# Softmax sums of a 12-head attention: inverted as 12 turned columns a group instead of 324, with the step lists in a new order

## Chip, core and metric

One core of one Trainium2 chip runs the whole program. The metric is the device time of one execution in microseconds. The engines named below are TensorE (PE, with its weight loads PEld), VectorE (DVE), ScalarE (ACT), GpSimd (POOL) and SyncE (SP), which issues most of the DMAs. Each takes its instructions strictly in the order of its own queue.

## What is computed

A batch of 32 images with text goes through a patch embedding, a causal single-head attention with rotary positions, a 12-head attention and a mixture of eight experts of which each token takes two. There are T = 324 tokens of D = 192 features, in three tiles of 108, and heads of 16 features.

```python
h = _L0_tok_ref(x, L0_tok_W, L0_tok_b)                 # patches @ W.T + b
h = jnp.concatenate([h, txt], axis=1)
h = h + _L0_attn_ref(_layernorm(h, axis=-1), L0_attn_Wq, L0_attn_Wk, L0_attn_Wv)
h = h + _L0_ffn_ref(_layernorm(h, axis=-1), ...)
# in _L0_ffn_ref, the part that the change touches:
qkv = (xn @ qkv_w.T + qkv_b).reshape(Bx, Nx, 3, H, hd).transpose(2, 0, 3, 1, 4)
q, k, v = (qkv[0], qkv[1], qkv[2])
attn = jax.nn.softmax(jnp.einsum('bhqd,bhkd->bhqk', q, k) * scale, axis=-1)
o = jnp.einsum('bhqk,bhkd->bqhd', attn, v).reshape(Bx, Nx, C)
x = x + (o @ proj_w.T + proj_b)
```

## The kernel before

The program is a pipeline over the 32 images. A turn works on several of them at once: the front (embedding, first attention, the q, k, v of the second) on image b, the back (scores, softmax and values of the second attention) on b - 1, the close (projection, gate, positions, scatter to the experts) on b - 2, and from turn 19 on the experts on tiles of 256 gathered tokens, three a turn. Turns 0 and 1 fill the pipeline, turns 2 to 18 have no experts (list ATTEND_STEPS), turns 19 to 31 have them (list BOTH_STEPS), two more turns of that list drain the pipeline, and a tile stage (TILE_STEPS) does the experts that are left. Before turn 18 VectorE also makes the tables of tiles (`tables`).

The order in which steps are issued is written out by hand in these lists. Every engine walks the same list and issues those of its steps in that order; a step waits on semaphores for what it reads, and a TensorE step also until its PSUM banks (ATTEND_BANKS, BOTH_BANKS, eight banks) have been read by the step that FREED names. A step late on TensorE's queue therefore holds up all behind it.

For the second attention the 12 heads are three groups of four; in a group each head owns 32 partitions. `s` (18 steps of two heads and one tile of queries) computes scores so that `mx` on VectorE can take row maxima; `mt` transposes the maxima of a group (three transposes), `nm` on ScalarE scales them. `st` (18 steps) computes the transposed scores with the maxima subtracted; two neighbouring steps of `s` or `st` use the two halves of the array's rows and overlap. `ex` on ScalarE takes the exponential of each. `pv` (three steps, L1692) multiplies with the values: the result of a group is a bank of 128 x 324, in which the 32 partitions of a head hold 16 rows of output and then rows of softmax sums, since the padding of `Vp` is ones. `no` (L1239, VectorE) divides: a stream shuffle copies the rows of sums over the partitions of each head (L1246), a reciprocal inverts all 128 x 324 of them (L1248), and a multiply by the bank gives Os (L1251). The last `no` of an image is followed by its projection `pj` in the next turn (L1704), which adds three groups; `pj`'s bank is freed by `x1`.

Other steps named later: `tr1`, `tr2`, `tr3` (transposes of normalized rows), `he`, `n0`, `n1`, `xf` (VectorE), `qk2`, `v2` (TensorE, q and k and v of the second attention), `qkh` (ScalarE, two activations L921 and L922), `v2e` (ScalarE), `gate` (TensorE, products of eight columns), `gt1` (VectorE, 14 small operations of the gating), `pos`, `rs` (GpSimd, rotary sums), `X`, `W1`, `ge` (Gelu), `W2`, `yv` of the experts, `ld`, `ad`, `scat` (loads of tiles, adds and scatters by DMA).

Of the kernel before, what the change touches and what calls it, by code (L numbers as in the profile page):

```python
# [5 lines left out]
ALU = mybir.AluOpType  # L6
# [1890 lines left out]
```

## Time and profile before

| | us |
|---|---|
| median of 3 runs | 2734.13 |
| lowest to highest | 2730.55 to 2734.61 |
| profiled execution | 2737.74 |
| its span, first to last instruction | 2735.9 |

The profile is of one execution. Its page gives each engine's busy time and the chain of work that ended last; the trace behind it can be asked for a stretch. A row of waits says which engine stood still, for whose result, how long in total, how many times, and the longest. A wait put down to "issue" is one for nothing that the profile shows. Times in rows are microseconds from the start of the span, the mean of one instruction is in ns, and PEclk is the granted TensorE clock as a share of the full one.

### The profile page before, as it was taken

How to read it: one execution, taken by the hardware profiler on the slowest of the kernel's cores; microseconds unless marked ns; L12 is line 12 of the kernel's file. 1: busy time of each engine (PE TensorE's matmuls, PEld its weight loads, DVE VectorE, ACT ScalarE, POOL GpSimd, SP SyncE). 2: the span in 40 equal slices, each digit the busy share in tenths (PEclk: the TensorE clock that was granted, in tenths of full speed). 3: DMA queues.
4: the chain of work that ended last, by engine and by line, in shares of the span. 5: the costliest groups of instructions: out<-in, count | busy, mean ns of one | idle time of the engine just before them, and what ended most of it. 6: DMA issues, size and time to landing. Idle time of an engine off the chain costs nothing.

```text
span 2735.9 us, 62967 instructions
## 1 busy us (share of the span) xinstructions
PE 2434.0 (89%) x19692; PEld 1899.6 (69%) x19692; DVE 1616.2 (59%) x4054; ACT 1163.4 (43%) x2242; POOL 1043.0 (38%) x1196
## 2 busy tenths in 40 slices
PE   3979999999999998999999999999998778788876
PEld 2846666666666666677777777777776567677776
DVE  2347888888888888766666766666665211110110
ACT  1223344434434443455555555555555223323332
POOL 1112333333333333344444444444443344444444
PEclk9669999999999999999999999999999789989998
DMA  6511312231232224354444444454433356756673
GB/s 106 168 21 29 50 30 34 38 49 30 34 49 37 34 35 59 104 114 112 112 110 111 108 105 102 97 111 112 110 94 97 94 158 186 193 162 189 167 196 101
DMA packets 251812, 263.21 MB, mean 96 GB/s; under 512 B 36156, under 2 KB 231464, under 8 KB 251752
## 3 DMA queue, kind: packets, MB, share of 16 engines
q1 hardware_dynamic: 214888, 230.18, 35.2%
q0 software_dynamic: 36864, 32.27, 6.6%
q8 instruction: 34, 0.56, 0.1%
q14 instruction: 26, 0.21, 0.0%
HBM read 212.43 MB, written 52.83 MB: 97 GB/s over the span
## 4 chain that ended last, share of the span: by engine, by line
PE 67%; issue 10%; DVE 9%; DMA 5%; ACT 3%; POOL 3%; SPq 2%; DVEq 0%; ACTq 0%; POOLq 0%
PE PS L1545 43%; PE PS L1700 7%; PE PS L1689 5%; DMA B2t<-in_L_ffn_b 4%; PE PS L1616 3%; DVE rsi L1248 3%; PE PS L1666 3%; DVE MX L1236 2%; PE PS L1739 1%; PE PS L1675 1%; ACT XE L966 1%; POOL tmp L733 1%; POOL tmp L734 1%; PE PS L1577 1%; ACT pool L946 1%
## 5 line engine op out<-in xcount | busy, mean ns | idle before, releaser
L1236 DVE TENSOR_REDUCE MX<-PS 108x2 f32<-108x648 f32 x576 | 456.5, 823 | 66.4 <-PE PS L1666 61.8
L796 POOL DMA_INDIRECT out<-big,tokn x192 | 303.4, 1580 | 480.0 <-DVE big L1385 324.7
L946 ACT ACTIVATE pool<-PS 108x648 f32<-108x648 f32 x576 | 383.6, 713 | 192.8 <-PE PS L1689 167.0
L1545 PE MATMUL PS<-WB,big 128*128 128x192 f32 x2304 | 432.8, 345 | 2.8 <-ACT big L975 2.8
L1545 PE MATMUL PS<-XE,WF 128*128 128x256 f16 x2880 | 370.2, 283 | 58.8 <-ACT XE L966 46.5
L975 ACT ACTIVATE big<-PS,WF 128x256 f32<-128x256 f32 x576 | 241.3, 470 | 404.7 <-PE PS L1545 403.0
L1545 PEld LDWEIGHTS PS<-WB,big 128*128 128x128 f32 x2304 | 401.3, 203 | 15.6 <-issue 6.6
L1545 PEld LDWEIGHTS PS<-XE,WF 128*128 128x128 f16 x2880 | 278.8, 101 | 132.4 <-ACT big L975 42.2
L1385 DVE SCALAR_TENSOR_TENSOR big<-PS,grow,GB 128x192 f32<-128x192 f32 x192 | 71.1, 412 | 459.3 <-PE PS L1545 459.3
L774 POOL DMA_INDIRECT xbuf<-XR,DST x192 | 190.5, 992 | 255.8 <-issue 216.0
L1248 DVE RECIPROCAL rsi<-rsi 128x324 f32<-128x324 f32 x96 | 209.1, 2178 | 3.3
L1700 PE MATMUL PS<-pool,Vp 108*32 108x324 f32 x2304 | 201.6, 489 | 0.0
L1545 PE MATMUL PS<-tokW,ximg 96*88 96x192 f32 (+1 forms) x1024 | 193.7, 349 | 1.2 <-DVE b1s L1462 1.2
L784 POOL TENSOR_SCALAR GB<-B2t,grow 128x192 f32<-128x192 f32 x192 | 163.0, 1055 | 72.8 <-DVE grow L1396 71.4
L1545 PEld LDWEIGHTS PS<-tokW,ximg 96*88 96x88 f32 (+1 forms) x1024 | 185.3, 255 | 4.7 <-issue 1.4
L1666 PE MATMUL PS<-KH,QA 32*108 32x324 f16 x1152 | 155.4, 339 | 35.1 <-ACT Vp L931 10.0
L1689 PE MATMUL PS<-QA,KH 32*108 32x324 f16 x1152 | 157.8, 346 | 15.9 <-DVE MX L1236 13.5
L966 ACT ACTIVATE XE<-PS 128x768 f16<-128x768 f16 x96 | 77.8, 810 | 194.4 <-PE PS L1739 194.3
L937 ACT ACTIVATE NM<-PS 128x324 f16<-128x324 f32 x96 | 42.2, 440 | 254.5 <-PE PS L1675 254.4
L1666 PEld LDWEIGHTS PS<-KH,QA 32*108 32x108 f16 x1152 | 60.0, 121 | 125.4 <-DVE MX L1236 38.0
L1689 PE MATMUL PS<-QA,KL 32*108 32x324 f16 x1152 | 143.8, 310 | 0.0
L1689 PE MATMUL PS<-NM,big 32*108 32x324 f16 x1152 | 143.6, 309 | 0.0
(209 smaller groups left out, 4142.4 us busy)
## 6 DMA issues: line engine op xcount, KB each, us to landing
WF<-w1p SPq DMA_DIRECT2D x96, 771.5 KB
WB<-in_L_ffn_W SPq DMA_DIRECT2D x96, 576.0 KB
ximg<-in_x SPq DMA_DIRECT2D x96, 196.0 KB
XtR<-xbuf SPq DMA_DIRECT2D x96, 196.0 KB
ximg<-in_x SPq DMA_DIRECT2D x96, 195.1 KB
B2t<-in_L_ffn_b SPq DMA_DIRECT2D x96, 96.0 KB
out<-R SPq DMA_DIRECT2D x32, 243.0 KB
w1p<-WF SPq DMA_DIRECT2D x8, 768.0 KB, 6.3
```

The source lines that it names most:

```text
L774: nc.gpsimd.indirect_dma_start(xbuf[:, :], bass.IndirectOffsetOnAxis(ap=DST[:, NT * k + t:NT * k + t + 1], axis=0), XR[:, t, :], None).the ...
L784: last = nc.gpsimd.tensor_scalar(GB[:, i % 2, s_, :], B2t[:, i, :], grow[:, i, s_:s_ + 1], None, ALU.mult)
L796: nc.gpsimd.indirect_dma_start(rows_out, bass.IndirectOffsetOnAxis(ap=tokn[:, i, s_:s_ + 1], axis=0), Yt[:, i, s_, :], None, bounds_check= ...
L946: nc.scalar.activation(Pr[:, at:at + 2, :], pair(("st", p))[0:TP, :, 0:T], ACT.Exp, scale=SCALE2).then_inc(S["ex"], 1)
L966: nc.scalar.activation(XE[:, i, :, :].rearrange("p k t -> p (k t)"), bank(("X", i))[:, 0:384].bitcast(F16), ACT.Copy).then_inc(S["x_evac"], 1)
L975: last = nc.scalar.activation(hid[:, i, c, :], ps[:, TILE * (c % 2):TILE * (c % 2) + TILE], ACT.Gelu, bias=WF1[:, i, 2 * HID + c:2 * HID + ...
L1236: nc.vector.tensor_reduce(MX[:, qt, g, 64 * jj:64 * jj + 64:32], pair(("s", p))[0:TP, :, 0:T], AX.X, ALU.max).then_inc(S["mx"], 1)
L1248: nc.vector.reciprocal(at, at).then_inc(S["inv"], 1)
L1545: last = nc.tensor.matmul(out_ap, lhsT, rhs, start=(i == 0), stop=(i == len(products) - 1))
L1666: last = nc.tensor.matmul(ps[0:TP, i, 0:T], QA[r, g, TP * qt:TP * qt + TP], KH[r, g, :], start=True, stop=True)
L1689: last = nc.tensor.matmul(ps[0:TP, i, 0:T], left[r], right[r], start=n == 0, stop=n == 2)
L1700: last = nc.tensor.matmul(ps[32 * j:32 * j + 32, 0:T], Vp[:, kt, 4 * g + j, :], Pr[:, at, :], start=kt == 0, stop=kt == NT - 1)
```

## The change

`no` is split over four engines, once for each group. `oe` (ScalarE) copies the bank of `pv` to Os, which frees the bank. `sx` (TensorE) transposes the three tiles of 108 tokens of Os into a bank of its own, so that a sum stands once per token and head, in one column of each head. `ri` (VectorE) inverts those 3 x 4 columns on 108 partitions into RC. `rx` (ScalarE) writes each inverse 32 times side by side into RX (108 x 3 x 128). `bx` (TensorE) transposes RX back to 128 x 324 in a bank, and `no` (VectorE) multiplies it by Os. So a batch has 18 steps of these six kinds in place of three of `no`. The buffer `rsi` goes; the tile tables that borrowed it borrow Nrm instead, and `tables` waits for `tr2` of the turn before.

Both lists are in a new order, with new banks. Tile stage, loads, first attention, scores, exponentials and experts are computed as before. Cut to its core (the lists by the ends of both turns):

```diff
-    mx=18, sums=3, inv=3, no=3, x1=1, cx=1, ...
+    mx=18, oe=3, sx=3, ri=3, rx=3, bx=3, no=3, x1=1, cx=1, ...
 ATTEND_STEPS = [
...
+    ("n3",), ("tr3",), ("mt", 2), ("ex", 9), ("xh",), ("st", 10), ("xm",), ("rcp",), ("h1",), ("st", 11), ("gate",),
+    ("ex", 10), ("nm", 2), ("st1",), ("st", 12), ("st", 13), ("ex", 11), ("ex", 12), ("ex", 13), ("st", 14), ("is1",),
+    ("pv", 1), ("st", 15), ("gt1",), ("ex", 14), ("n1",), ("oe", 1), ("st", 16), ("st", 17), ("ex", 15), ("sx", 0),
+    ("ri", 0), ("pos",), ("tr2",), ("ex", 16), ("sx", 1), ("ex", 17), ("th",), ("tr2h",), ("xf",), ("ri", 1),
+    ("rx", 0), ("pv", 2), ("tr2l",), ("bx", 0), ("oe", 2), ("rx", 1), ("qk2", 0), ("xl",), ("no", 0), ("pos2",),
+    ("bx", 1), ("qk2", 1), ("qkh", 0), ("gt2",), ("scat",), ("hb",), ("qkh", 1), ("keep",), ("no", 1), ("sx", 2),
+    ("qkl", 0), ("ri", 2), ("rx", 2), ("qk2", 2), ("bx", 2), ("qkh", 2), ("qkl", 1), ("no", 2), ("v2",), ("v2e",),
+    ("qkl", 2),
 ]
...
+    ("gate",): (5,) ... ("sx", 0): (5,),
...
 BOTH_STEPS = [
...
+    ("qkh", 0), ("bx", 0), ("qk2", 1), ("no", 0), ("qkl", 0), ("ad", 2), ("qkh", 1), ("pv", 2), ("qk2", 2), ("rx", 1),
+    ("bx", 1), ("oe", 2), ("sx", 2), ("qkl", 1), ("ri", 2), ("qkh", 2), ("rx", 2), ("v2",), ("v2e",), ("qkl", 2),
+    ("bx", 2), ("no", 1), ("no", 2),
 ]
-         "qk2": "qkl", "v2": "v2e", "s": "mx", "mt": "nm", "st": "ex", "pv": "no", "pj": "x1", "tr3": "xm",
+         "qk2": "qkl", "v2": "v2e", "s": "mx", "mt": "nm", "st": "ex", "pv": "oe", "sx": "ri", "bx": "no", "pj": "x1", "tr3": "xm",
-        rsi = sb("rsi", [128, 2, T], F32)
+        RC = sb("RC", [TP, NT, HEADS], F32)
+        RX = sb("RX", [TP, NT, 128], F32)
+            def oe(b, g):
+                act.wait_ge(S["pv"], due("pv", b, g + 1))
+                act.wait_ge(S["pj"], due("pj", b - 1, 1))
+                nc.scalar.activation(Os[:, g, :], bank(("pv", g))[:, 0:T], ACT.Copy).then_inc(S["oe"], 1)
+            def rx(b, g):
+                act.wait_ge(S["ri"], due("ri", b, g + 1))
+                act.wait_ge(S["bx"], due("bx", b, g))
+                apart(act)
+                nc.scalar.activation(RX[:, :, :].rearrange("p t (j r) -> p t j r", j=4),
+                                     RC[:, :, 4 * g:4 * g + 4].rearrange("p t (j r) -> p t j r", r=1).to_broadcast(
+                                         [TP, NT, 4, 32]), ACT.Copy).then_inc(S["rx"], 1)
+            def ri(b, g):
+                dve.wait_ge(S["sx"], due("sx", b, g + 1))
+                dve.wait_ge(S["rx"], due("rx", b - 1, g + 1))
+                sums = bank(("sx", g))[0:TP, 0:384].rearrange("p (t j r) -> p t j r", t=NT, j=4)[:, :, :, HD]
+                nc.vector.reciprocal(RC[:, :, 4 * g:4 * g + 4], sums).then_inc(S["ri"], 1)
             def no(b, g):
-                nc.vector.stream_shuffle(at, ps, [16 + i % 16 for i in range(32)]).then_inc(S["sums"], 1)
-                nc.vector.reciprocal(at, at).then_inc(S["inv"], 1)
-                nc.vector.tensor_tensor(Os[:, g, :], ps, at, ALU.mult).then_inc(S["no"], 1)
+                dve.wait_ge(S["bx"], due("bx", b, g + 1))
+                nc.vector.tensor_tensor(Os[:, g, :], bank(("bx", g))[:, 0:T], Os[:, g, :], ALU.mult).then_inc(S["no"], 1)
-                dve.wait_ge(S["no"], due("no", attended, 3))
+                dve.wait_ge(S["tr2"], due("tr2", turned_, 1))
+            def sx(turn, b, g):
+                pe.wait_ge(S["oe"], due("oe", b, g + 1))
+                free(pe, turn, ("sx", g))
+                ps = bank(("sx", g))
+                for t in range(NT):
+                    last = nc.tensor.transpose(ps[0:TP, 128 * t:128 * t + 128], Os[:, g, TP * t:TP * t + TP], ident)
+                last.then_inc(S["sx"], 1)
+            def bx(turn, b, g):
+                pe.wait_ge(S["rx"], due("rx", b, g + 1))
+                free(pe, turn, ("bx", g))
+                ps = bank(("bx", g))
+                for t in range(NT):
+                    last = nc.tensor.transpose(ps[:, TP * t:TP * t + TP], RX[:, t, :], ident[0:TP, 0:TP])
+                last.then_inc(S["bx"], 1)
```

## Rows read from the trace of the kernel before

**Rows 1.** The page: busy time by engine, and the chain that ended last.

```profile
PE 2434.0 (89%) x19692; PEld 1899.6 (69%) x19692; DVE 1616.2 (59%) x4054; ACT 1163.4 (43%) x2242; POOL 1043.0 (38%) x1196
PE 67%; issue 10%; DVE 9%; DMA 5%; ACT 3%; POOL 3%; SPq 2%; DVEq 0%; ACTq 0%; POOLq 0%
```

**Rows 2.** Stretches by stage: us, busy by engine, clock, DMA share, GB/s.

```profile
213.10:1075.90 862.80, 807.33 (x6851) 569.78 (x6849) 734.23 (x1743) 355.34 (x720) 287.11 (x380) 0.95 0.25 38
1075.90:1139.70 63.80, 53.37 (x431) 38.33 (x429) 54.18 (x132) 22.21 (x45) 21.21 (x27) 0.87 0.60 143
1139.70:1999.40 859.70, 833.73 (x7298) 656.94 (x7297) 587.51 (x1482) 478.48 (x863) 381.39 (x429) 0.99 0.47 106
2136.00:2735.90 599.90, 472.20 (x3280) 427.12 (x3280) 75.23 (x324) 180.10 (x382) 267.27 (x233) 0.88 0.59 163
```

**Rows 3.** The same view of single turns: two of ATTEND, one of BOTH.

```profile
541.92:594.71 52.79, 49.39 (x431) 35.30 (x429) 46.05 (x110) 22.21 (x45) 18.19 (x24) 0.97 0.25 39
...
648.00:702.30 54.30, 50.99 (x431) 35.85 (x429) 45.94 (x109) 22.21 (x45) 18.19 (x24) 0.94 0.25 38
...
1283.62:1354.86 71.24, 69.10 (x611) 54.37 (x609) 49.22 (x125) 39.90 (x73) 32.11 (x37) 1.00 0.47 107
```

**Rows 4.** Waits of TensorE's weight loads, 213.1 to 1075.9 us (16 ATTEND turns).

```profile
PEld PS L1689 <- DVE MX L1236: 20.8, 48, 0.6
...
PEld PS L1545 <- DVE tmp L1196: 3.8, 16, 0.2
...
PEld PS L1689 <- ACT pool L946: 3.0, 16, 0.2
```

**Rows 5.** The same waits, 1139.7 to 1999.4 us (12 BOTH turns).

```profile
PEld PS L1577 <- ACT pool L946: 9.0, 12, 0.9
...
PEld PS L1675 <- DVE Os L1251: 7.8, 12, 0.7
...
PEld PS L1700 <- DVE MX L1236: 0.2, 1, 0.2
```

**Rows 6.** VectorE's groups by line: shapes, count, busy us, mean ns, idle before.

```profile
L1248 DVE RECIPROCAL rsi<-rsi 128x324 f32<-128x324 f32 x96 | 209.1, 2178 | 3.3
...
L1246 DVE STREAM_SHUFFLE rsi<-PS 128x324 f32<-128x324 f32 x96 | 50.1, 522 | 1.1 <-issue 0.4
...
L1251 DVE TENSOR_TENSOR Os<-PS,rsi 128x324 f32<-128x324 f32 x96 | 47.6, 496 | 3.3
...
L1212 DVE RECIPROCAL nm<-nm 108x3 f32<-108x3 f32 x32 | 5.4, 170 | 0.0
```

**Rows 7.** TensorE in order of time, BOTH: start, us, instruction.

```profile
1328.17 0.44 PE L1675 MATMUL PS<-cst,MX 108*128 108x108 f32 x3
1328.55 0.34 PE L1666 MATMUL PS<-KH,QA 32*108 32x324 f16 x2
...
1353.29 0.41 PE L1545 MATMUL PS<-qkvWa,XT 128*108 128x192 f16 x3
...
1354.53 0.50 PE L1739 MATMUL PS<-id,XtR 128*128 128x128 f16 x6
```

**Rows 8.** ScalarE's groups by line.

```profile
L921 ACT ACTIVATE qm<-PS,qmb,cst 128x324 f16<-128x324 f32 x96 | 59.6, 621 | 74.4 <-PE PS L1545 74.4
...
L937 ACT ACTIVATE NM<-PS 128x324 f16<-128x324 f32 x96 | 42.2, 440 | 254.5 <-PE PS L1675 254.4
...
L957 ACT ACTIVATE XR<-NB 108x576 f16<-108x576 f32 x32 | 22.3, 696 | 0.0
```

**Rows 9.** An ATTEND turn around its low clock: two stretches, and TensorE's `gate`.

```profile
573.35:580.18 6.83, 6.50 (x65) 4.51 (x63) 6.08 (x15) 5.86 (x10) 3.41 (x6) 1.00 0.00 0
580.18:583.59 3.41, 3.41 (x30) 2.25 (x33) 3.10 (x12) 0.33 (x1) 2.65 (x4) 0.50 0.24 73
...
578.48 1.77 PE L1545 MATMUL PS<-gateW,XM 128*108 128x8 f32 x12
```

**Rows 10.** ScalarE's table loads, 1139.7 to 1999.4 us (12 BOTH turns).

```profile
L975 ACT ACT_TABLE_LOAD x36 | 46.2, 1283 | 76.8 <-PE PS L1545 76.6
```

More of the change, by code:

```diff
@@ L73 @@
     nm=3, ex=18, xm=1, xh=1, th=1,
-    mx=18, sums=3, inv=3, no=3, x1=1, cx=1, ch=1, var3=1, n3=1, logit=1, hot=1, tin=1, gt2=1, pos2=1, bstep=BACK_STEPS,
+    mx=18, oe=3, sx=3, ri=3, rx=3, bx=3, no=3, x1=1, cx=1, ch=1, var3=1, n3=1, logit=1, hot=1, tin=1, gt2=1, pos2=1, bstep=BACK_STEPS,
     rr=1, eps3=1, is3=1, xl=1, scat=96)
@@ L82 @@
     SP=("xin", "text", "keep", "tin0", "tin1", "tin2"),
-    PE=("emb", "tr1", "qk1", "v1", "s1", "p1t", "pv1", "tr2", "qk2", "v2", "s", "mt", "st", "pv", "pj", "tr3", "gate",
+    PE=("emb", "tr1", "qk1", "v1", "s1", "p1t", "pv1", "tr2", "qk2", "v2", "s", "mt", "st", "pv", "sx", "bx", "pj", "tr3", "gate",
         "pos", "x_full", "w1", "o_full"),
-    ACT=("tr1h", "v1e", "e1", "p1e", "tr2h", "qkh", "v2e", "nm", "ex", "xm", "xh", "th", "x_evac", "gelu"),
-    DVE=("he", "var0", "n0", "tr1l", "rm", "m1", "rcp", "h1", "var1", "n1", "xf", "tr2l", "qkl", "fstep", "mx", "sums",
-         "inv", "no", "x1", "var3", "n3", "logit", "hot", "tin", "gt2", "pos2", "bstep", "y_done", "gs", "gm"),
+    ACT=("tr1h", "v1e", "e1", "p1e", "tr2h", "qkh", "v2e", "nm", "ex", "oe", "rx", "xm", "xh", "th", "x_evac", "gelu"),
+    DVE=("he", "var0", "n0", "tr1l", "rm", "m1", "rcp", "h1", "var1", "n1", "xf", "tr2l", "qkl", "fstep", "mx", "ri",
+         "no", "x1", "var3", "n3", "logit", "hot", "tin", "gt2", "pos2", "bstep", "y_done", "gs", "gm"),
     POOL=("eps0", "is0", "rs", "eps1", "is1", "hb", "cx", "ch", "rr", "eps3", "is3", "xl", "gb"))
@@ L190 @@
             "v2e", "xin", "text"}
-IN_BACK = {"s", "mx", "mt", "nm", "st", "ex", "pv", "no", "cx", "ch"}
+IN_BACK = {"s", "mx", "mt", "nm", "st", "ex", "pv", "oe", "sx", "ri", "rx", "bx", "no", "cx", "ch"}
 IN_EXPERT = {"X", "xe", "W1", "ge", "W2", "yv", "ad", "ld", "gm", "gb"}
@@ L375, in build_program @@
         toh = X1[:, :, :].rearrange("p t d -> p (t d)")[:, 0:NTL * E].rearrange("p (n e) -> p n e", n=NTL)
-        tbs = rsi[0:TP, :, :].rearrange("p a t -> p (a t)")
+        tbs = Nrm[:, :, :].rearrange("p t d -> p (t d)")
         tb8 = tbs[:, 0:6 * E].rearrange("p (a e) -> p a e", e=E)
@@ L1004, in run @@
                         ex(b, step[1])
+                    elif kind == "oe":
+                        oe(b, step[1])
+                    elif kind == "rx":
+                        rx(b, step[1])
                     elif kind == "xm":
@@ L1237, in mx @@
                                         ALU.max).then_inc(S["mx"], 1)
-            def no(b, g):
-                dve.wait_ge(S["pv"], due("pv", b, g + 1))
-                dve.wait_ge(S["no"], due("no", b, g))
-                apart(dve)
-                ps = bank(("pv", g))[:, 0:T]
-                at = rsi[:, g % 2, :]
-                nc.vector.stream_shuffle(at, ps, [16 + i % 16 for i in range(32)]).then_inc(S["sums"], 1)
-                dve.wait_ge(S["sums"], due("sums", b, g + 1))
-                nc.vector.reciprocal(at, at).then_inc(S["inv"], 1)
-                dve.wait_ge(S["inv"], due("inv", b, g + 1))
-                dve.wait_ge(S["pj"], due("pj", b - 1, 1))
-                nc.vector.tensor_tensor(Os[:, g, :], ps, at, ALU.mult).then_inc(S["no"], 1)
+            def ri(b, g):
[3 more added lines that the diff above has]
+                nc.vector.reciprocal(RC[:, :, 4 * g:4 * g + 4], sums).then_inc(S["ri"], 1)
+            def no(b, g):
+                dve.wait_ge(S["bx"], due("bx", b, g + 1))
+                nc.vector.tensor_tensor(Os[:, g, :], bank(("bx", g))[:, 0:T], Os[:, g, :], ALU.mult).then_inc(S["no"], 1)
             def x1(b):
@@ L1331, in row, with tables @@
                 return cst[0:TP, c:c + n]
-            def tables(g, attended):
+            def tables(g, turned_):
                 def wide_e(ap, n):
@@ L1438, in run @@
                         mx(b, step[1])
+                    elif kind == "ri":
+                        ri(b, step[1])
                     elif kind == "no":
@@ L1466, in _ @@
                 run(Turn(ATTEND, Batch(b), Batch(b) - 1, Batch(b) - 2, None))
-            tables(0, LAG - 3)
+            tables(0, LAG - 2)
             run(Turn(ATTEND, LAG - 1, LAG - 2, LAG - 3, None))
@@ L1801, in run @@
                         pv(turn, b, step[1])
+                    elif kind == "sx":
+                        sx(turn, b, step[1])
+                    elif kind == "bx":
+                        bx(turn, b, step[1])
                     elif kind == "pj":
```

111 rows, old and new, of tables (ATTEND_BANKS, ATTEND_STEPS, BOTH_BANKS, BOTH_STEPS) are left out of this document.

## The prediction

> **What bounds the kernel now.** I read the engine totals first: TensorE is busy 89% of the span, VectorE 59%, ScalarE 43%, and the chain of work that ended last is 67% TensorE and 9% VectorE [rows 1]. These are means over stages, so next comes the table by stage [rows 2]. Seventeen attention turns (ATTEND list) run from 213 to 1140 us: sixteen take 862.8 us, 53.9 each, with TensorE at 94% and VectorE at 85%, and the seventeenth, which also makes the tile tables, 63.8. Thirteen mixed turns (BOTH list) follow; twelve of them take 859.7 us, with TensorE at 97% and VectorE at 68%. Behind 2136 us lies the tile stage, 599.9 us, in which the change touches nothing. Single turns [rows 3] show that the pattern repeats to 0.01 us in BOTH, and in ATTEND to the length of a stretch of low clock.
>
> So TensorE's in-order queue is the path, and what counts is why it stands still. The waits of its weight loads name a producer. In the sixteen ATTEND turns 13 such rows add up to 119.7 us, 7.5 a turn; six of them name VectorE (73.8 us, 4.6 a turn), mostly a bank of scores that `mx` has yet to reduce [rows 4]. In twelve BOTH turns nine rows add up to 48.4 us, 4.0 a turn, 2.4 of them on VectorE; 0.65 a turn is TensorE standing behind the last multiply of `no` [rows 5]. A part of each such wait is the hand-over itself and can't go.
>
> **What leaves VectorE.** Each head group's `no` is a shuffle, a reciprocal over 324 columns and a multiply: 522 + 2178 + 496 ns, 3.20 us [rows 6]. Three groups make 9.6 us of a turn's 46.0. The multiply stays. The reciprocal shrinks to 12 columns on 108 partitions: between the 3-column row (170 ns) and the 324-column row lie 6.3 ns a column, so 170 + 9 x 6.3 = 0.23 us [rows 6]. The new cost is 3 x (0.23 + 0.50) = 2.2 us, and VectorE loses 7.4 us a turn: 38.6 of about 53 in ATTEND, 41.8 of 71 in BOTH.
>
> **What comes to TensorE.** `sx` and `bx` are three fp32 transposes each, 18 more matmuls a batch. The nearest step is `mt`, three transposes, 0.38 us from its start (1328.17) to that of the next step (1328.55) [rows 7]. `bx` has just its shape; `sx` streams 128 columns where `mt` streams 108, so at most 0.45. The sum is 3 x (0.38 + 0.45) = 2.5 us when each hand-over is paid; without any the six steps would be about 1.8. Most of the new steps stand beside other full-array products, so I take 2.2 us a batch. None of it lies beside other TensorE work: it is on the path in full, 32 batches x 2.2 = 70 us if nothing is given back. This cost is certain, the gain isn't.
>
> **What comes to ScalarE.** `oe` copies 128 x 324 out of PSUM: 440 ns by `nm` [rows 8]. `rx` writes 108 x 384 from SBUF: between that and the 576-column SBUF copy (0.70 us), so 0.5. Three of both add 2.9 us a turn, to 22.2 in ATTEND and 39.9 in BOTH [rows 3]: hidden as busy time. As latency it isn't. The old chain was pv, 3.2 us on one engine, pj. The new one is pv, oe, sx, ri, rx, bx, no: 0.44 + 0.45 + 0.23 + 0.5 + 0.38 + 0.5 = 2.5 us and five more hand-overs between engines, each behind whatever is queued there. In return the `pv` bank is free after a copy of 0.44 us instead of 3.2. The switches between exp and gelu tables cost 1.28 us each, three pairs a BOTH turn [rows 10]; counting `ge` against `ex` and `e1` in the new list gives three pairs again, so 0. The other operations of both lists are the same, DMA loads and scatters too; `ld`, `ad` and `scat` move by a few steps in queues whose waits TensorE's rows don't name, so 0, and up to 0.5 us a turn if a tile load is then late for `X`. The order of `s` and `st` steps that overlap in the two halves of the array is as good as it was: I count 12 serial units of `st` in ATTEND before and after, 10 in BOTH; `s` has 13, then 12, and 11, 11. So reordering by itself is worth at most 0.2 us there.
>
> **What waits are added.** In ATTEND `sx` of group 0 takes the bank of `gate`, which is free only after the last of the gating's 14 small VectorE operations; `st` 12 to 17 and `pv` 1 cover them. I allow it up to 0.5 us, an estimate from the longest waits for a bank in these turns, and `pos`, `tr2` and everything behind stand with it. In BOTH the last three groups are crowded at the turn's end: `rx` 2 (0.5) is queued on ScalarE behind `qkh` 2 (0.62 us [rows 8] and a second activation like it), some 1.7 us, while only `v2` covers it, 1.24 us from 1353.29 to 1354.53 [rows 7]. So `bx` 2 may stand 0.5 us just ahead of the next turn's first product.
>
> **What is given back.** For ATTEND the bounds are 0 and 7.5 us a turn. With VectorE at 38.6 of 53 (73%) it is loaded as VectorE is in BOTH now (69%), and BOTH shows 4.0 us of named waits; I take that: 3.5 us back, net 2.2 - 3.5 = -1.3 us a turn. For BOTH the bounds are 0 and 4.0; I let the 0.65 behind `no` go and half of the other 1.75 on VectorE, 1.5 us, net +0.7. What is late next in ATTEND is the exp queue, `v2e` and the rotary sums on GpSimd. The sum: 17 x -1.3 = -22, 13 x +0.7 = +9, and +3 for the first and the two drain turns, where the longer chain has little cover. Together -10 us on the profiled 2737.7 us, so 2728; the median shown lies 3.6 us under that profile, so 2724.
>
> **A rule weighed against the trace.** In each ATTEND turn there is one stretch at the lower of the two clock levels: here 3.4 us at 0.50 right behind the 12 eight-column products of `gate`, with the transposes of `tr3` shortly before them, with 1.00 before and after; the turns of 54.3 us have it twice as long [rows 3, 9]. The change puts more transposes into the turn. The Trainium skill (TensorE: Matmul & The Clock Gate, section on PE-mode transpose) says that transposes don't count as busy for the clock in the way other matmuls do. By that the low stretch would grow; the trace agrees only in the place where it begins, which has the tiny products as well. The skill's Perfetto Trace Analysis (Identifying the Most-Contended Engine) says to work on the engine with the highest occupancy first; here the change unloads the second and loads the first.
>
> **Rivals.** First, slower: TensorE's order decides. The waits of BOTH are hand-overs and ScalarE's, not VectorE's load, so the 2.2 us stay whole there and the crowded end adds 0.3; in ATTEND just the 2.2 added comes back. That is 13 x 2.5 + 3 = +35 on the profiled time: 2769 as a median; with nothing back in ATTEND either, 17 x 2.2 more: 2806. It decides if less than 2.2 us of the 4.0 in BOTH and of the 7.5 in ATTEND goes. For it: TensorE at 97% in BOTH, where two fifths of the named waits (19.8 of 48.4 us) are on ScalarE. Against: VectorE is named in 4.6 of 7.5 us in ATTEND [rows 4]. Second, the relief works in full: ATTEND loses the 4.6 on VectorE and half the rest (net -3.8), BOTH 3 of its 4.0 (net -0.8): 17 x -3.8 + 13 x -0.8 + 3 = -72, 2662; halfway from my case, 2693. For it: 85% of VectorE in ATTEND. Against: most of the waits on `mx` lie in the first half of the turn, where no step of `no` stands but the tail of the last turn's. Third, the low clock grows in ATTEND: 3.4 us more at half speed in each of 17 turns cost 1.7 each, +29 on my sum: 2753. For it the transposes and the place; against it that BOTH, with transposes too, runs at 1.00 [rows 3]. Fourth, the reciprocal isn't short in its new shape, and VectorE keeps its 6.5 us a turn: then nothing comes back and all of the 70 us stay: 2804. The 3-column row speaks against it.
>
> **How the numbers follow.** My case, 2705 to 2740: 0.38. TensorE's order: 0.30. Full relief: 0.18. Low clock: 0.10. The fourth: 0.04. The range reaches from the way to full relief, 2690, to a little past the first rival, 2780. A change of 0.2% (5.5 us) is about what a measurement here can tell from none; my case lies with 0.26 below that band, 0.09 in it and 0.03 above, and the two middle rivals leave 0.04 more in it. Faster 0.26 + 0.18 = 0.44; same 0.13; slower 0.43.
>
> **What would show it.** Right: the reciprocal row at about 0.23 us x96 and no shuffle; VectorE at 38 to 39 us in an ATTEND turn; ATTEND turns of 52 to 53 us with VectorE's waits near 2 us; BOTH turns of 71.5 to 72.5. Wrong: BOTH turns of 73.5 or more with TensorE still at 97% (first rival), or below 71 (second); more than one low stretch a turn or a granted clock under 0.93 in ATTEND (third). Rows of TensorE standing for `oe` or `rx` would say that the chain, not the load, is the new bound.

## The result, and the profile after

The changed kernel takes 2792.3 us, the median of 4 runs (2789.1 to 2794.5), beside 2732.3 us (2728.9 to 2734.6) for the kernel before. The ratio is 1.022, 95% interval 1.0202 to 1.0237: slower by 60 us, outside the forecast range. The profiled execution took 2794.5 us.

First the page of the changed kernel, engines and chain, which answers [rows 1].

```profile
PE 2490.5 (89%) x20268; PEld 1948.5 (70%) x20268; DVE 1424.9 (51%) x3862; ACT 1258.9 (45%) x2434; POOL 1043.8 (37%) x1196
PE 76%; issue 6%; DVE 5%; DMA 5%; ACT 3%; SPq 2%; POOL 1%; DVEq 0%; ACTq 0%; POOLq 0%
```

VectorE lost 191.3 us of work and ScalarE gained 95.5. TensorE still has 89% of a longer span, and the chain that ended last has 76% of it instead of 67%. Next the stages, with the columns of [rows 2]: fifteen ATTEND turns, the sixteenth and the seventeenth (which share the work of the tile tables now), twelve BOTH turns, and what follows the last of them.

```profile
220.40:1019.20 798.80, 757.09 (x6691) 552.41 (x6691) 584.20 (x1546) 378.13 (x765) 268.20 (x357) 0.96 0.25 38
1019.20:1077.90 58.70, 50.14 (x449) 36.68 (x447) 44.24 (x122) 25.21 (x51) 20.66 (x27) 0.93 0.26 41
1077.90:1134.40 56.50, 53.47 (x449) 39.46 (x449) 38.15 (x108) 25.40 (x52) 16.15 (x22) 0.89 0.64 150
1134.40:2067.00 932.60, 898.78 (x7515) 690.03 (x7513) 539.11 (x1412) 515.89 (x937) 390.77 (x435) 0.95 0.44 99
2067.00:2792.60 725.60, 582.60 (x4361) 511.61 (x4359) 144.28 (x513) 257.34 (x517) 319.21 (x288) 0.92 0.55 151
```

The seventeen turns before 1134.4 take 914.0 us instead of 926.6 [rows 2]: 12.6 gained. The twelve BOTH turns take 932.6 instead of 859.7, 72.9 lost. Their clock is 0.95 instead of 0.99. The rest nearly cancels: the first turn is 6.2 us longer, the second 2 shorter, the start 3 later, and the stretch behind the last full turn 10.9 shorter. That last stretch lies between 721 and 738 us in all profiled executions of this study, whatever was changed in the lists, so no cause is read into it.

Two single BOTH turns of the changed kernel, and in them two stretches of the second [rows 3 has the turn of before].

```profile
1209.53:1283.75 74.22, 71.24 (x628) 55.91 (x626) 45.14 (x118) 42.70 (x79) 32.41 (x36) 1.00 0.47 104
1674.60:1753.09 78.49, 75.65 (x628) 57.77 (x626) 45.18 (x118) 43.02 (x79) 32.36 (x36) 0.93 0.44 99
1704.94:1708.35 3.41, 3.41 (x26) 2.20 (x23) 0.00 (x0) 2.16 (x4) 2.03 (x2) 0.50 0.00 0
1728.83:1735.66 6.83, 6.83 (x47) 3.40 (x43) 3.50 (x15) 3.99 (x6) 2.84 (x3) 0.50 0.29 29
```

The same work takes 74.22 us at the higher of the two clock levels and 78.49 where 10.2 us of the turn are granted the lower one. Nine of the twelve turns are of the second kind. Their low clock is in two pieces: 3.4 us that begin 30.3 us into the turn, and 6.8 us that begin 54.2 us into it, 0.4 us behind the twelve eight-column products of `gate` (52.2 to 53.8 us into the turn). The second piece is the same kind of place that [rows 9] shows for ATTEND. In the kernel before a BOTH turn without low clock took 71.24 [rows 3], and only three of twelve had a stretch of 3.4 us.

Why TensorE stands, in seven of the long turns (1439.1 to 1988.6 us), is in its waits. The two longest of the named rows are shown; [rows 5] has neither wait.

```profile
PEld PS L1697 <- DVE MX L1260: 9.6, 7, 1.4
PEld PS L1610 <- DVE tmp L1220: 6.8, 7, 1.0
```

`mt` stands 1.4 us a turn for the maxima of VectorE, `tr3` 1.0 for the rotary products. VectorE has less to do than before, so something holds it up. Here are VectorE, GpSimd and then TensorE in order of time (start, us, instruction, count, idle before and its cause), in the second of the two turns above.

```profile
1696.35 1.56 DVE L1220 TENSOR_TENSOR tmp<-PS,cst 96x648 f32<-96x648 f32 x2
1697.83 3.79 DVE L1204 TENSOR_SCALAR NB<-X,mvb,rsb 108x192 f32<-108x192 f32 x3
1701.55 0.82 DVE L1260 TENSOR_REDUCE MX<-PS 108x2 f32<-108x648 f32 x1
...
1695.95 1.65 POOL L803 DMA_INDIRECT out<-big,tokn  x1 [4.24 <-DVE big L1405]
1697.90 1.58 POOL L803 DMA_INDIRECT out<-big,tokn  x1 [0.30 <-issue]
1698.90 1.48 POOL L740 TENSOR_TENSOR tmp<-tmp 96x324 f32<-96x324 f32 x1
1699.74 1.47 POOL L741 TENSOR_TENSOR tmp<-tmp 96x324 f32<-96x324 f32 x1
...
1702.42 0.78 PE L1697 MATMUL PS<-cst,MX 108*128 108x108 f32 x6 [1.10 <-DVE MX L1260]
1703.97 0.77 PE L1610 MATMUL PS<-cst,NB 108*128 108x108 f32 x6 [0.78 <-DVE tmp L1220]
```

The row to look at is L1204, `n3`: three instructions take 3.79 us. The next view shows the three, first in the changed kernel, then in the same turn place of the kernel before (min, median and longest in ns, then when the first and the last of them started).

```profile
L1204 DVE TENSOR_SCALAR NB<-X,mvb,rsb x3: 365/370/3215, 1697.8 to 1701.3; 108x192 f32<-108x192 f32 x3
```

```profile
L1180 DVE TENSOR_SCALAR NB<-X,mvb,rsb x3: 370/377/378, 1318.0 to 1318.5; 108x192 f32<-108x192 f32 x3
```

The second of the three takes 3215 ns, from 1698.12 to 1701.33, and it ends 0.13 us behind the last of GpSimd's four operations; the first issue had ended before it began. In the new BOTH list `ad` 0 (the scatter whose issue is DMA_INDIRECT, L803) stands ahead of `rs` and `n3`, and `n3` stands beside both. That is a long way from the old list, where `n3` was 87th, behind both `rs`, and `ad` 0 125th of 194 steps; now `ad` 0 is 53rd and `n3` 66th of 209. The maxima and rotary products queued behind `n3` on VectorE are what TensorE then waits for. The first low stretch begins at 1704.94, right behind these two waits. The Trainium skill (SBUF — State Buffer, section "Who interferes with whom") says that VectorE in its two-port modes and GpSimd take one pair of ports as an exclusive lock, for whole instructions. The trace agrees on the waiting: one instruction is held to the end of the others' work, while two keep their 0.37 us. That `n3` runs in a two-port mode is not shown: its 370 ns for 192 columns are not below the 348 ns that VectorE takes for a sum of 192 columns with one input in PSUM (L1281).

### The profile page after: what moved, and what is told of

The parts are those of the page before. It is cut to its first block, busy times and chain, and to the rows that moved or that the text cites. A ratio compares the mean times of both kernels' runs of the same rounds, so it can differ in the third digit from the quotient of the medians.

```text
span 2792.6 us, 64688 instructions
## 1 busy us (share of the span) xinstructions
PE 2490.5 (89%) x20268; PEld 1948.5 (70%) x20268; DVE 1424.9 (51%) x3862; ACT 1258.9 (45%) x2434; POOL 1043.8 (37%) x1196
## 4 chain that ended last, share of the span: by engine, by line
PE 76%; issue 6%; DVE 5%; DMA 5%; ACT 3%; SPq 2%; POOL 1%; DVEq 0%; ACTq 0%; POOLq 0%
PE PS L1567 47%; PE PS L1711 7%; PE PS L1722 7%; DMA B2t<-in_L_ffn_b 4%; PE PS L1638 3%; PE PS L1688 3%; DVE MX L1260 2%; PE PS L1777 1%; PE PS L1731 1%; ACT XE L986 1%; PE PS L1739 1%; PE PS L1599 1%; PE PS L1649 1%; DVE tmp L1220 1%; ACT pool L953 1%
## 5 line engine op out<-in xcount | busy, mean ns | idle before, releaser
L803 POOL DMA_INDIRECT out<-big,tokn x192 | 305.3, 1590 | 369.7 <-DVE big L1405 219.4
L1567 PE MATMUL PS<-XE,WF 128*128 128x256 f16 x2880 | 381.5, 289 | 57.0 <-ACT XE L986 46.1
L1567 PE MATMUL PS<-WB,big 128*128 128x192 f32 x2304 | 424.9, 340 | 2.8 <-ACT big L995 2.8
L1567 PEld LDWEIGHTS PS<-WB,big 128*128 128x128 f32 x2304 | 391.0, 198 | 20.7 <-issue 10.0
L1567 PEld LDWEIGHTS PS<-XE,WF 128*128 128x128 f16 x2880 | 286.8, 103 | 121.0 <-ACT big L995 40.0
L1722 PE MATMUL PS<-pool,Vp 108*32 108x324 f32 x2304 | 210.1, 506 | 1.6 <-ACT pool L953 1.5
L1688 PE MATMUL PS<-KH,QA 32*108 32x324 f16 x1152 | 145.5, 335 | 18.4 <-DVE MX L1260 5.8
L740 POOL TENSOR_TENSOR tmp<-tmp 96x324 f32<-96x324 f32 x64 | 66.3, 1036 | 201.3 <-DVE tmp L1220 201.3
L1722 PEld LDWEIGHTS PS<-pool,Vp 108*32 108x32 f32 x2304 | 72.8, 122 | 98.3 <-issue 54.2
```

The costliest lines, as they stand in the source:

```text
L803: nc.gpsimd.indirect_dma_start(rows_out, bass.IndirectOffsetOnAxis(ap=tokn[:, i, s_:s_ + 1], axis=0), Yt[:, i, s_, :], None, bounds_check= ...
L1567: last = nc.tensor.matmul(out_ap, lhsT, rhs, start=(i == 0), stop=(i == len(products) - 1))
L1688: last = nc.tensor.matmul(ps[0:TP, i, 0:T], QA[r, g, TP * qt:TP * qt + TP], KH[r, g, :], start=True, stop=True)
L1722: last = nc.tensor.matmul(ps[32 * j:32 * j + 32, 0:T], Vp[:, kt, 4 * g + j, :], Pr[:, at, :], start=kt == 0, stop=kt == NT - 1)
```

## The experiments

All ran beside the kernel before, whose medians in the three groups of runs were 2731.9, 2732.7 and 2732.4 us. Theory A is that the new order of BOTH makes the loss, by `n3` beside GpSimd and the low clock that comes with it, with a price of some 2 us a turn for the turned sums. The main rival is that the transposes themselves make it.

**`n3` earlier.**

```diff
-    ("yv", 0), ("qk1", 0), ("ad", 0), ... ("ge", 1, 0), ("n3",), ("mx", 12),
+    ("yv", 0), ("n3",), ("qk1", 0), ("ad", 0), ... ("ge", 1, 0), ("mx", 12),
```

> The changed kernel with one step moved in the BOTH list: n3 (three multiplies of VectorE over SBUF) stands right behind yv 0 instead of behind rm 0 and ge 1 0, so that it runs before GpSimd reaches the add of tile 0 and the rotary sums. In the changed kernel the three take 3.79 us in a BOTH turn instead of 0.95, mt then waits 1.10 us for mx and tr3 0.78 us for rm, and a stretch of 3.4 us at clock 0.50 follows. Theory A (the order of the BOTH list costs the time, by this collision and the low clock behind it): n3 back at about 1 us, both waits gone, the first low stretch gone, BOTH turns 3 to 4 us shorter (75 us), total 2740 to 2755. Rival B (the 18 transposes cost it, by themselves and by the clock): n3 is short, but the low stretches stay and the total falls by no more than 20 us.

Measured: 2746.4 us (2745.6 to 2747.9), ratio 1.0067 (1.0041 to 1.0093). One VectorE step moved by a few places in the list gives back 46 of the 60 us. `n3` is at its old length again, as the groups by line show over all turns:

```profile
L1204 DVE TENSOR_SCALAR NB<-X,mvb,rsb 108x192 f32<-108x192 f32 x96 | 30.4, 372 | 0.0
```

A BOTH turn without low clock, in the view of single turns, takes 73.12 us:

```profile
1202.95:1276.07 73.12, 71.27 (x628) 56.08 (x627) 42.54 (x119) 42.72 (x79) 32.40 (x36) 1.00 0.48 106
```

The twelve BOTH turns have a mean of 73.81 us with 2.0 us of low clock a turn, not 8.5. The piece at 30 us is gone from all of them, and the later one, now 52 to 54 us into the turn, is 3.4 us long in seven turns and gone in five. TensorE's busy time in a turn without low clock is as in the changed kernel (71.27 and 71.24 us), so the 1.1 us between 74.22 and 73.12 are waits.

**`ad` 0 later**, behind `rs` 1, with `n3` where the change put it.

```diff
-    ("yv", 0), ("qk1", 0), ("ad", 0), ("X", 1), ... ("rs", 1), ("ge", 1, 2),
+    ("yv", 0), ("qk1", 0), ("X", 1), ... ("rs", 1), ("ad", 0), ("ge", 1, 2),
```

> The changed kernel with the indirect add of tile 0 moved behind rs 1 on GpSimd's queue in the BOTH list. It tells what stretches n3. If it is the add of tile 0 (1695.95 to 1699.48 us in the turn looked at), n3 is back at 1 us and the total falls by some 40 us. If it is the rotary sums rs 0, which now start at once behind rm 0, n3 stays at 2.5 us or more and the total within 10 us of the changed kernel's 2792. By rival B nothing moves by more than 20 us either way.

Measured: 2740.5 us (2729.3 to 2756.5), ratio 1.0021 (0.9998 to 1.0044). This one step gives back 52 of the 60 us, with `n3` in the place where the change put it. Neither expectation had that: `n3` isn't back at 1 us, and yet the time fell. The three of `n3` and the one wait of TensorE behind them, over some eight turns (1439 to 1988 us):

```profile
L1204 DVE TENSOR_SCALAR NB<-X,mvb,rsb 108x192 f32<-108x192 f32 x24 | 16.4, 736 | 0.0
PE PS L1610 <- DVE tmp L1220: 2.9, 8, 0.4
```

`n3` takes 3 x 0.736 = 2.2 us, at 1677 us 0.36, 0.92 and 0.92, the last two beside the two operations of `rs` 0. So the rotary sums stretch it too, but TensorE then stands 0.36 us at `tr3` and not at all at `mt`, where it stood 0.78 and 1.10. What costs TensorE its time is the issue of `ad` 0 beside `n3`, not the stretch by `rs` alone. The low stretch at 30 us into the turn is gone; that at 51 us (6.8 us long) stays in each turn, and BOTH turns take 75.1. But its profiled execution, 2756.5 us, is the longest of its ten, so these turns are not those of its median.

**The old BOTH list with the turned sums put into it.**

```diff
     ("pv", 0), ("W1", 2, 2), ("ex", 7),
+    ("oe", 0), ("sx", 0),
     ("ge", 2, 2), ("gate",), ("is1",),
+    ("ri", 0),
...
+    ("rx", 0), ... ("bx", 0), ... ("no", 0), ... ("oe", 1), ... ("sx", 1), ... ("ri", 1), ... ("rx", 1), ... ("bx", 1),
...
+    ("oe", 2), ... ("sx", 2), ... ("ri", 2), ... ("rx", 2), ... ("bx", 2), ("no", 2),
```

> The new arithmetic in full, the new ATTEND list, but the BOTH list of the kernel before with the 18 steps set in between (sx in the bank that pv leaves, bx in banks 5, 0 and 1). Theory A: only the work of the transposes is left, BOTH turns of 72.5 to 74 us at clock 1.00, ATTEND turns 52.9 us, total 2735 to 2755. Rival B: low stretches appear in this list too, BOTH turns of 76 us or more, total over 2770.

Measured: 2754.6 us (2747.7 to 2756.9), ratio 1.0098 (1.0071 to 1.0125). BOTH turns without low clock take 74.39 us, their mean is 74.93, and `n3` is 371 ns. So the turned sums cost 3.15 us a turn when they are put in at these places, against 1.9 with the new order mended (73.12 - 71.24). The new order isn't bad as such: it is 1.3 us better than this one placement and then loses more at one place. The first turn, which also runs the BOTH list, is back to 83.3 us here, so its 6 us were the new list's too.

**Every transpose twice.** `sx` and `bx` issue each of their transposes two times, 36 a batch instead of 18, with the same result.

```diff
-                for t in range(NT):
+                for t in 2 * list(range(NT)):
```

> The changed kernel with every transpose of sx and bx done twice, 36 instead of 18 in a batch. It prices the transposes. Theory A: the second set costs its own 1.8 us in a turn, all of it on TensorE's path, 30 turns: +55 us, 2845, with the low stretches as long as before. Rival B: the low stretches grow too, by another 3.4 us at half clock in a turn or more, +100 us or over.

Measured: 2797.8 us (2787.2 to 2803.7), ratio 1.0248. ATTEND turns grow by 1.3 us. BOTH turns without low clock take 75.65 instead of 74.22, so 18 more transposes are worth 1.4 us when they stand right behind the others, without hand-overs of their own. The time is 5.5 us over the changed kernel's, where both expectations had 50 or more. But with twice the transposes the low clock of the BOTH turns goes from 8.5 us a turn to 1.1, and the twelve turns are shorter together than the changed kernel's 932.6 us:

```profile
1153.13:2066.90 913.77, 876.90 (x7731) 695.65 (x7729) 538.22 (x1412) 511.33 (x937) 390.31 (x434) 0.99 0.45 101
```

That speaks against transposes as the cause of the low clock. It also says that a stall like that of `n3`, which is still there (1.10 and 0.78 us), doesn't bring the low stretch by itself: what else stands around it matters.

**The change in ATTEND only.** ATTEND has the new list and the turned sums, BOTH its old list and old arithmetic (the lines of the list are left out here).

```diff
+            def no(b, g):
+                if plan[0] is not ATTEND:
...
+                    nc.vector.stream_shuffle(rsi[:, :], ps, [16 + i % 16 for i in range(32)]).then_inc(S["sums"], 1)
+                    nc.vector.reciprocal(rsi[:, :], rsi[:, :]).then_inc(S["inv"], 1)
+                    nc.vector.tensor_tensor(Os[:, g, :], ps, rsi[:, :], ALU.mult).then_inc(S["no"], 1)
+                    return
```

> The changed list and the turned sums only in the ATTEND turns; the BOTH turns have their old list and the old shuffle, reciprocal over 324 columns and multiply. Theory A (all of the loss is made in BOTH, and the ATTEND turns keep their small gain whatever stands behind them): ATTEND turns 2 to 16 at a mean of 53.2 to 53.5 us, turns 2 to 18 together 10 to 14 us shorter than before, BOTH turns at 71.6 as before, the time 2716 to 2724 us, ratio 0.994 to 0.997. Rival B (the transposes bring the low clock wherever they stand): more low clock in ATTEND than the 4 to 6 us a turn seen so far, no gain: 2732 or more.

Measured: 2721.6 us (2714.0 to 2731.0, 12 runs), ratio 0.996 (0.9943 to 0.9976). It is faster than both kernels, than the one before by 0.4%. Fifteen ATTEND turns and twelve BOTH turns of it, in the view by stage:

```profile
217.80:1018.70 800.90, 756.06 (x6691) 551.62 (x6691) 581.78 (x1546) 378.14 (x765) 268.43 (x357) 0.96 0.25 38
1130.51:1990.61 860.10, 833.99 (x7299) 657.14 (x7297) 587.37 (x1482) 479.37 (x863) 383.23 (x430) 0.99 0.47 106
```

ATTEND turns have a mean of 53.39 us, BOTH turns are at 71.68 as before. All of the loss is made in turns that run the new BOTH list.

**The wide step ahead of `gate`.** The kernel with `ad` 0 later, and `W1` 2 2 moved ahead of the tiny products.

```diff
-    ("ld", 1), ("gate",), ... ("nm", 2), ("W1", 2, 2), ("gt1",), ("pv", 1), ("ge", 2, 2), ("pos",), ...
+    ("ld", 1), ("W1", 2, 2), ("gate",), ... ("nm", 2), ("gt1",), ("pv", 1), ("ge", 2, 2), ... ("pos",), ("pos2",), ("W2", 2, 0)
```

> The kernel of e2_ad0_late, and in BOTH the wide product step W1 2 2 stands ahead of gate instead of behind it, and pos with pos2 two steps further back, so that the eight-column products of gate no longer follow sx 0 and its hand-over directly. e2 had one low stretch of 6.8 us in each BOTH turn, at 50.7 us into it, behind this place. Theory A (a low stretch follows where TensorE has stood and then runs small products): the stretch goes or halves, BOTH from 75.1 to 72 to 74 us, the time 2710 to 2730. Rival B (the transposes set the clock, whatever lies around them): the stretch stays, BOTH 75 us, 2735 to 2745.

Measured: 2751.4 us (2743.9 to 2758.8), ratio 1.0069 (1.0042 to 1.0097), so against the two medians no gain. In the profile the stretch at 51 us shrank from 6.8 to 3.4 us in six turns, was gone in five and grew to 10.2 in one, and the BOTH turns have a mean of 73.97 instead of 75.11. It now lies about 54 us into the turn. The time of the program is 11 us over that of its base. The profile of the base is its longest run (2756.5 us) and this one is a run of 2750.6 us, near its median, so the two sets of turns can't be compared finely, and that the turns gained isn't shown. It stays open.

**`n3` against GpSimd in the kernel before.** Two tries to put the suspected cost into the kernel before, without any turned sums. In the first, `n3` came right behind `rm` 0.

```diff
-    ("rm", 0), ("rm", 1), ("rs", 0), ... ("st", 2), ("n3",), ("st", 3),
+    ("rm", 0), ("n3",), ("rm", 1), ("rs", 0), ... ("st", 2), ("st", 3),
```

> The kernel before with one step moved in BOTH: the three n3 instructions of VectorE come right behind rm 0, so that they run beside GpSimd's rotary sums, with no turned sums anywhere. Theory A (n3 is stretched by GpSimd's work beside it, and TensorE then waits): n3 at 0.7 to 1.3 us each instead of 0.37, BOTH turns 0.5 to 1.5 us longer, with a low stretch behind the stalls 3 us or more; the time 2740 to 2775. Rival B (the stretched n3 is a by-effect and only the new steps cost): n3 stretched or not, BOTH within 0.3 us of 71.65 and the time within 5 us of before.

Measured: 2810.6 us (2804.7 to 2821.4), ratio 1.0294 (1.0259 to 1.0328), more than expected, and by another way. `is3`, whose factors `n3` needs, stood later in GpSimd's queue. `n3` kept its 0.37 us but stood 3.1 us for it, `rm` 1 stood behind, and TensorE had one stall, here in order of time:

```profile
1709.59 0.33 PE L1545 MATMUL PS<-attWb,XT 128*108 128x192 f16 x2
1713.24 0.51 PE L1666 MATMUL PS<-KH,QA 32*108 32x324 f16 x2 [3.33 <-DVE tmp L1196]
```

The turn around it:

```profile
1684.13:1762.64 78.51, 72.70 (x612) 56.25 (x609) 48.27 (x125) 40.02 (x73) 32.15 (x37) 0.93 0.44 98
```

Of the 7.3 us over the turn of [rows 3] the stall is 3.3. The rest is low clock: 10.2 us a turn at 0.50, from 1712.38 to 1722.62 us, and TensorE's busy time grew by 3.6 us with the work unchanged. The stretch begins 0.9 us before the stall ends (1713.24).

In the second try `is3` was moved forward too, so that `n3` finds its factors ready and runs beside `rs`.

```diff
-    ("st3",), ("W2", 0, 0), ... ("rm", 0), ("rm", 1), ("rs", 0), ... ("is3",), ... ("n3",),
+    ("st3",), ("is3",), ("W2", 0, 0), ... ("rm", 0), ("rm", 1), ("n3",), ("rs", 0), ...
```

> The kernel before, with its BOTH list changed at two steps: is3 (GpSimd) comes right behind st3, and n3 (VectorE) right behind rm 1, so that n3 finds its factors ready and runs beside GpSimd's rotary sums rs 0. In e7 n3 stood 3.1 us a turn for is3 and was not stretched, TensorE stood 3.3 us in one piece, and BOTH went to 78.5 us with 10.2 us of low clock in each turn. Theory A (a VectorE step of this kind takes longer while GpSimd works on SBUF, and the length of the one stall decides over the clock): n3 at 0.5 to 1.1 us each instead of 0.37, no stall over 1.5 us, BOTH 71.5 to 73, the time 2730 to 2752. Rival B (n3 is stretched as in the changed kernel, to 3 us for one, by the rotary sums alone): BOTH 74 to 78, the time 2760 to 2810. Rival C (no stretch without the indirect DMA that stands in GpSimd's queue in the changed kernel): n3 at 0.37 to 0.40, BOTH 71.2 to 71.9.

Measured: 2801.0 us (2793.7 to 2804.5), ratio 1.0251 (1.0226 to 1.0276): by itself the move of two steps costs the kernel before more than the whole change did (68.6 against 60 us).

The three of one turn, GpSimd in order of time beside them, and two turns, the second of which holds them:

```profile
L1180 DVE TENSOR_SCALAR NB<-X,mvb,rsb x3: 365/923/1521, 1697.5 to 1698.7; 108x192 f32<-108x192 f32 x3
```

```profile
1697.71 0.94 POOL L733 TENSOR_TENSOR tmp<-tmp 96x324 f32<-96x324 f32 x1 [0.21 <-DVE tmp L1196]
1698.61 0.88 POOL L734 TENSOR_TENSOR tmp<-tmp 96x324 f32<-96x324 f32 x1
```

```profile
1368.42:1443.77 75.35, 70.14 (x612) 54.91 (x609) 49.74 (x125) 39.98 (x73) 32.24 (x37) 0.98 0.43 100
1672.34:1750.33 77.99, 73.11 (x612) 56.65 (x609) 49.74 (x125) 40.07 (x73) 32.24 (x37) 0.93 0.44 98
```

`n3` is stretched to 0.92 us beside the rotary sums, and to 1.52 us beside the last of them and the copy `cx` behind it; it ends 0.11 us behind that copy. So GpSimd stretches `n3` without an indirect DMA, and rival C falls. One of the three is longer than theory A had it (0.5 to 1.1 us), and the effect is much larger: the time lies where rival B put it, without its 3 us for one. TensorE stands up to 2.8 us in one piece, and its busy time again grows, by 1.0 us in turns with a low stretch of 3.4 us and by 4.0 in those with 10.2. How far the stall comes from the stretch (2.65 us for the three instead of 0.95) and how far from `n3` now standing ahead of the maxima isn't separated.

**The turned sums in the old ATTEND list**, BOTH as before, in two placements. The diff is between the two, at the end of the turn: in the second, `rx` 2 stands ahead of `qkh` 2 and `no` 2 behind the last `qkl`.

```diff
-    ("pv", 2), ("oe", 2), ("qk2", 2), ("sx", 2), ("ri", 2), ("v2",), ("bx", 2), ("no", 2), ("qkl", 1), ("hb",), ("qkh", 2), ("rx", 2), ("qkl", 2)
+    ("qk2", 2), ("pv", 2), ("oe", 2), ("qkl", 1), ("sx", 2), ("v2",), ("ri", 2), ("hb",), ("rx", 2), ("qkh", 2), ("bx", 2), ("qkl", 2), ("xf",), ("no", 2)
```

> As e5_hybrid, with the old ATTEND list and the new steps (oe, sx, ri, rx, bx and no) put into it near their old places. It tells the new order from the new arithmetic in ATTEND. Theory A (the relief of VectorE makes the gain, the order of the other steps is worth 0.2 us a turn at most): ATTEND 53.2 to 53.7 us, the time 2716 to 2728. Rival B (the new order makes the gain, the arithmetic alone costs its 1.3 to 2 us on TensorE): ATTEND 54.5 to 56, the time 2740 to 2765.

> As e9_hyb_attold, but the steps of head group 2 put better: rx 2 ahead of qkh 2 on ScalarE, no 2 behind the last qkl on VectorE, so that no engine stands behind the chain of the turned sums. In e9 VectorE stood 82 us in 13 turns for the embedding and TensorE for KL and H, with 14.6 us of low clock a turn. Theory A (e9 lost by my placing; the turned sums themselves gain in ATTEND by VectorE's relief): ATTEND 53 to 54.5 us with 3 to 6 us of low clock, the time 2715 to 2740. Rival B (in the old order the longer chain of the sums can't be hidden, the new order is what makes the gain): ATTEND 56 or more, the time over 2765.

Measured: 2863.4 us (ratio 1.047, 1.0436 to 1.0504) and 2840.2 us (1.0403, 1.0361 to 1.0444). ATTEND turns have a mean of 62.0 and 60.8 us, of which 14.6 and 12.4 are at low clock; BOTH turns are at 71.9 in both. Both lie above all that was expected of the first; the expectation that a better placing would bring 53 to 54.5 us fell, and its rival (56 or more, over 2765) held. The longest waits of VectorE in the second (300 to 1100 us, thirteen turns; total, times, longest):

```profile
DVE RC L1269 <- PE PS L1748: 62.6, 26, 3.0
DVE H L1146 <- PE PS L1584: 61.4, 13, 6.3
DVE Os L1285 <- PE PS L1756: 35.1, 27, 2.1
DVE Nrm L1189 <- POOL rsf L728: 31.5, 13, 2.4
```

VectorE stands 4.8 us a turn for the transposed sums, 4.7 for the embedding, 2.7 for the transposed inverses and 2.4 for `n1`'s factors from GpSimd. So in ATTEND the arithmetic without the new order loses, in the two placements tried. Whether a third, or other banks for the six new steps, would do as well as the new list wasn't tried.

**Both mendings of the BOTH list**, `n3` early and `W1` 2 2 ahead of `gate`, in the changed kernel.

```diff
+    ("yv", 0), ("n3",), ("qk1", 0), ("ad", 0), ...
+    ("ld", 1), ("W1", 2, 2), ("gate",), ... ("hb",), ("pos",), ("pos2",), ("W2", 2, 0)
```

> The changed kernel with both mendings of its BOTH list: n3 right behind yv 0 as in e1, and W1 2 2 ahead of gate with pos later as in e6. Theory A (the two low stretches of a turn each follow one place in the order): BOTH turns 72.5 to 73.5 us with under 1.5 us of low clock, what is left over the old 71.65 being the price of the turned sums on TensorE; the time 2728 to 2745. Rival B (mending one place moves the stretch to another): BOTH 73.8 or more as in e1 and e6, 2746 or more. Under 72 us a turn would say that the turned sums cost nothing in BOTH, and the time would be under 2722.

Measured: 2761.6 us (2750.5 to 2769.1), ratio 1.0112 (1.0084 to 1.0139). BOTH turns have a mean of 74.69 us; without low clock they take 73.5, and a stretch of 3.4 us lies 54 to 55 us into seven of the twelve (one more has 10.2). The mendings don't add: all four runs of the two together are longer than all four of `n3` alone, though the intervals of the two ratios overlap a little. The rival's numbers (73.8 or more, 2746 or more) hold here.

## Why the prediction was wrong, step by step

**The loss, by its parts.** A BOTH turn went from 71.65 to 77.72 us, by 6.07. Turns without low clock tell the parts: 71.24 before, 73.12 with `n3` early, 74.22 as changed. So the turned sums, with the rest of the new order, cost 1.88, `n3` beside GpSimd 1.10, and the low clock 3.50 (77.72 - 74.22) instead of 0.41 (71.65 - 71.24), 3.09 more. The last two are 4.2 of the 6.07, and moving `n3` took away 3.9 of them (77.72 - 73.81). Only 3.4 of the 10.2 us of low clock begin behind the stall of `n3`; the other 6.8 begin behind `gate`, 24 us later. Why those shrink when `n3` moves isn't shown.

**The step that failed: "`ld`, `ad` and `scat` move by a few steps ..., so 0".** I priced the move by the DMAs alone and bounded it by a late tile load. It isn't a few steps either: `ad` 0 went from the 125th place of the BOTH list to the 53rd, and `n3` from behind `rs` 1 to ahead of `rs` 0. `ad` 0 is also 1.6 us of GpSimd's time for each issue, and it now stands beside `n3`. In place of the 0 the runs showed 52 us of the program for `ad` 0 (moved behind `rs` 1, `n3` left where it was) and 46 us for `n3` (moved ahead of both): two ways to take one collision apart. The row that I should have asked for is GpSimd's queue around every VectorE step whose place changes. That TensorE's waits didn't name GpSimd before was no reason: GpSimd acts on VectorE, VectorE on TensorE. I also looked for a bad order only among `s` and `st`, and left out the other VectorE steps; that is the second half of the same failure ("reordering by itself is worth at most 0.2 us there").

**The low clock: a part of the loss, but not where and not by what the rival had it.** The third rival put it in ATTEND, by the transposes, at +29 us. It went down there, from 5.9 to 4.1 us a turn, and grew in BOTH from 0.9 to 8.5. That BOTH ran at 1.00 I took as evidence against; it was so for BOTH in its old order alone, and there three turns of twelve were 1.5 to 1.7 us longer with a stretch of low clock, so "repeats to 0.01 us in BOTH" held for nine. The rule of the Trainium skill on transposes (TensorE: Matmul & The Clock Gate, section on PE-mode transpose) isn't what decides here: with twice the transposes the low clock of BOTH nearly went, and in the kernel before it came to 10.2 us a turn with no transpose added.

**BOTH's price of the sums.** Forecast 2.2 - 1.5 = +0.7; measured +1.9 at best and +3.15 in the old order. The 2.2 stands: in turns without low clock TensorE's busy time went from 69.10 to 71.27 us with `n3` early, 2.17 more (transposes and order are not told apart in it; the second set of transposes, without hand-overs, was 1.3 to 1.4, against my 1.8). The give-back of 1.5 was the error: the time in which TensorE isn't busy went from 2.14 to 1.85 us, so 0.3 came back. The 0.65 us behind `no` did go, but others came: with `n3` early the weight loads wait 26.9 us for VectorE in twelve BOTH turns, against 28.6 before. The first rival was right that the waits of BOTH are not VectorE's load.

**ATTEND.** Forecast -1.3 a turn. Measured over the same seventeen turns -0.74 (-12.6 / 17), the right sign and half the size; its turns of 52.9 lie where forecast. The waits of TensorE on VectorE fell from 4.6 to 3.9 us a turn (62.5 us in sixteen turns), not to near 2. That was the term that was too large: with VectorE at 39 us of 53 the waits on `mx` in the first half of a turn stay, as the second rival's "against" says. That reordering is worth at most 0.2 us doesn't stand here either: in the old order the sums lose 7 to 8 us a turn.

**What held.** The durations: `ri` 0.23 us forecast and measured, `oe` 0.44 and 0.44, `rx` 0.5 and 0.52, `no` 0.5 and 0.49.

```profile
L1267 DVE RECIPROCAL RC<-PS 108x12 f32<-108x12 f32 x96 | 22.2, 231 | 89.5 <-PE PS L1731 89.5
L959 ACT ACTIVATE Os<-PS 128x324 f32<-128x324 f32 x96 | 42.3, 441 | 92.8 <-PE PS L1722 92.6
L965 ACT ACTIVATE RX<-RC 108x384 f32<-108x384 f32 x96 | 50.2, 523 | 2.0 <-DVE RC L1267 1.1
L1271 DVE TENSOR_TENSOR Os<-PS,Os 128x324 f32<-128x324 f32 x96 | 46.1, 492 | 31.2 <-PE PS L1739 30.9
```

VectorE's load fell as said. Where I had feared the crowded end of BOTH, no row shows a wait of size for `rx` 2. Every price of an operation on VectorE and ScalarE was right; the range failed on what stands beside what. The named waits that I treated as the whole room for gain and loss can't show a wait that a new neighbour makes.

**What is settled and what is open.** Shown: all of the loss is made by the new BOTH list; 46 of 60 us go with the place of `n3`, 52 with that of `ad` 0; a VectorE step beside GpSimd is stretched, also in the kernel before, and stalls of 2.5 us and more come with low clock there. Not settled: which combination around a stall brings the low clock, since with doubled transposes the same stall brought little of it, why the stretch behind `gate` shrinks when `n3` moves, and why the two mendings don't add. `n3` early and `ad` 0 late in one kernel wasn't tried.

## What to carry to other kernels

When a hand-written order changes, lay GpSimd's queue beside VectorE's for every step that moves, indirect DMA issues included: an instruction of 0.37 us became one of 3.2. In a stage that TensorE fills to 97%, allow for more than the length of a stall, since low clock can come with it (3.3 us of stall cost 7.3 here, while two of 1.1 and 0.8 us came with no low clock in eight of twelve turns where the transposes were doubled), and try a change stage by stage, since the one that lost 6 us a turn in BOTH gained in ATTEND.

## What the runs showed of the hardware

A VectorE instruction of 370 ns took 3215 ns beside one DMA_INDIRECT issue and two tensor operations of GpSimd, and the latter show 1.48 and 1.47 us there, against 0.94 and 0.88 in the last experiment on `n3`. Each stretched instruction of `n3` looked at ends 0.11 to 0.13 us behind the end of a GpSimd operation. VectorE's rotary products, which read PSUM and a table, kept their 0.82 us beside the first DMA_INDIRECT (1696.35 us in the turn shown). Turns settle at fixed lengths: the last nine of the twelve BOTH turns of the changed kernel take 78.37 to 78.52 us, and the last eight of the kernel before with `n3` behind `rm` 0 take 78.50 to 78.55. In both, 10.2 us of the turn are at the lower clock level, whose share was 0.50 in every stretch looked at.
